# Layer normalisations of a feed-forward stage moved to ScalarE, attention masks cut to the outer thirds, and keys folded in 32-column pieces

## The reference, cut to what matters

```
def _layernorm(x, g, b): return (x - mu) * rsqrt(var + EPS) * g + b
valid = (abs(rel) <= w) & (k_pos >= 0) & (k_pos < S)
scores = where(valid, scores, -1e9); p = softmax(scores)
x = _layernorm(src + attn, ln1_g, ln1_b)
ff = maximum(x @ W1 + b1, 0.0) @ W2 + b2
return _layernorm(x + ff, ln2_g, ln2_b)
...
x = _layernorm(x + attention_layer(x))
q = einsum(x, w_q); q = (q - mean) * rsqrt(var + BN_EPS) * gamma + beta
sim = einsum('pbnhd,hkpd->pbnhk', q, keys)
```

## Time and profile before

| | us |
|---|---|
| median of 3 runs | 786.74 |
| lowest and highest | 784.21, 788.45 |
| profiled execution, its own time | 785.28 |
| span in the profile | 783.4 |
| busy PE, DVE, POOL, ACT | 624.2, 617.0, 435.2, 334.5 |

### The profile page before, as it was taken

One profiled execution on the slowest core, in us unless ns is written; L12 is line 12 of the kernel. 1 busy time (PEld: TensorE's weight loads), 2 busy tenths in 40 slices (PEclk: granted clock), 3 DMA queues, 4 the chain that ended last, 5 costly groups with the idle time before them and its releaser, 6 DMA issues.

```text
span 783.4 us, 46593 instructions
## 1 busy us (share of the span) xinstructions
PE 624.2 (80%) x19753; PEld 517.8 (66%) x19783; DVE 617.0 (79%) x1903; ACT 334.5 (43%) x514; POOL 435.2 (56%) x672
## 2 busy tenths in 40 slices
PE   5889989999988977877847487787877777777775
PEld 4667768778876855554645376676766666666674
DVE  3656747776766757999965888899999999999982
ACT  3434534545444452433320434455555455455540
POOL 4222422333232423554521778879888888898881
PEclk9999999999999998988975789999999999999997
DMA  6511111111111110000000122312222222222221
GB/s 171 196 32 38 30 29 30 37 33 35 33 36 28 34 54 14 15 28 13 0 8 3 40 62 64 70 41 67 67 67 67 64 64 67 67 67 51 58 61 41
DMA packets 45361, 38.81 MB, mean 50 GB/s; under 512 B 6512, under 2 KB 40432, under 8 KB 45040
## 3 DMA queue, kind: packets, MB, share of 16 engines
q1 hardware_dynamic: 45296, 37.86, 19.1%
HBM read 16.86 MB, written 2.10 MB: 24 GB/s over the span
## 4 chain that ended last, share of the span: by engine, by line
PE 41%; DVE 39%; issue 16%; POOL 1%; DVEq 1%; ACT 1%; DMA 1%; another core or an unknown queue 1%; SPq 0%; POOLq 0%; ACTq 0%
PE ps L640 12%; PE ps L653 8%; DVE top L1226 5%; PE ps L666 5%; DVE wq_sb L1257 4%; DVE prod L1281 3%; PE ps L635 3%; PE ps L806 3%; PE ps L827 3%; DVE hidT L1272 3%; DVE best L1237 2%; DVE stats L1040 2%; DVE x L1057 2%; DVE r_x L1266 2%; DVE r L1057 2%
## 5 line engine op out<-in xcount | busy, mean ns | idle before, releaser
L999 DVE TENSOR_REDUCE row_max<-ps 128x8 f32<-128x768 f32 x64 | 61.3, 958 | 77.2 <-PE ps L640 77.2
L827 PE MATMUL ps<-up_sb,prod 128*128 128x128 f32 x512 | 81.4, 322 | 46.7 <-DVE prod L1281 46.3
L462 POOL COPY v_ones<-v_raw 96x512 f32<-96x512 f32 x32 | 19.5, 609 | 168.5 <-DMA v_raw<-in_x_wrapped 168.5
L827 PEld LDWEIGHTS ps<-up_sb,prod 128*128 128x128 f32 x512 | 75.0, 229 | 53.4 <-DVE prod L1281 53.2
L864 ACT ACTIVATE arena<-arena 128x768 f32<-128x768 f32 x64 | 54.0, 844 | 125.9 <-DVE arena L1002 125.9
L640 PE MATMUL ps<-early 128*32 128x96 f32 x4096 | 102.4, 250 | 6.3 <-issue 6.3
L640 PEld LDWEIGHTS ps<-early 128*32 128x32 f32 x4096 | 86.8, 111 | 29.1 <-issue 29.1
L806 PE MATMUL ps<-arena,hidT 128*32 128x32 f32 x8192 | 82.0, 200 | 25.5 <-issue 20.8
L806 PEld LDWEIGHTS ps<-arena,hidT 128*32 128x32 f32 x8192 | 76.9, 112 | 31.0 <-issue 22.2
L557 POOL TENSOR_TENSOR wq_sb<-wq_sb,rel_exp 128x1024 f32<-128x1024 f32 x32 | 76.2, 2380 | 8.2 <-POOL rel_exp L553 7.2
L653 PE MATMUL ps<-ident,arena 128*96 128x128 f32 x512 | 70.0, 280 | 12.9 <-issue 7.6
(11 more groups left out here) (138 smaller groups left out, 1275.4 us busy)
## 6 DMA issues: line engine op xcount, KB each, us to landing
arena<-r_x SPq DMA_DIRECT2D x128, 128.0 KB, 2.4
v_raw<-in_x_wrapped SPq DMA_DIRECT2D x128, 48.0 KB, 1.8
arena<-in_x SPq DMA_DIRECT2D x8, 256.0 KB, 5.1
x_tile<-in_x SPq DMA_DIRECT2D x32, 64.0 KB, 1.8
x<-in_x SPq DMA_DIRECT2D x8, 256.0 KB, 2.8
xT_tile<-xT SPq DMA_DIRECT2D x32, 64.0 KB, 1.9
out<-out_tile SPq DMA_DIRECT2D x32, 64.0 KB, 1.5
wq_sb<-in_w_q SPq DMA_DIRECT2D x1, 1024.0 KB, 9.6
```

The lines of the kernel that those rows point to most:

```text
L827: mm = nc.tensor.matmul(ps[:, 6 + p, 0:P], pairs[:, c // 2, c % 2], up_sb[:, c, :], start=False, stop=(c == EC - 1))
L999: V.tensor_reduce(mx.rearrange("p (a b) -> p a b", a=2), sc, AX_X, ALU.max).then_inc(max_done, 1)
```

## The change

Three things are changed.

1. *Attention*: the mask matmuls come after the scores and cover only the outer thirds of each window, 256 columns in place of 384. The first score matmuls open the banks.
2. *Feed-forward*: (x - mean) * rstd becomes an ACTIVATE Identity with a scale and a shift column on ScalarE (`normalised`, four of 128x128 per norm). VectorE writes also -mean (`minus_mean`), GpSimd multiplies it by rstd (`ln_shift`) behind each power. VectorE keeps the multiply by g and the add (`ln1_affine`, `ln2_affine`; norm 3 has neither).
3. *Middle*: w_sim's products are cut into four 32-column pieces each, written to four 32-partition strips. The constant row of the first part goes to bank 0, so its splitting starts while TensorE still works on the second (`split_constants`), and ScalarE copies w_sim.

```diff
+        minus_mean = sb("minus_mean", [P, 12])
+        ln_shift = sb("ln_shift", [P, 12])
...
+                pool.wait_ge(rstd_done, k + 1)
+                hold(pool)
+                nc.gpsimd.tensor_tensor(ln_shift[:, 4 * lo:4 * hi], minus_mean[:, 4 * lo:4 * hi], rstd[:, 4 * lo:4 * hi],
+                                        ALU.mult).then_inc(shift_ready, 1)
...
-                for g in groups:
-                    nc.tensor.matmul(ps[:, g, 0:BLOCKS * WIN], ident_bf[:], mask[:, mask_at], start=True, stop=False,
-                                     skip_group_check=True)
                 for b in range(BLOCKS):
                     for g in groups:
                         for h in range(4):
                             mm = nc.tensor.matmul(ps[32 * h:32 * h + 32, g, b * WIN:(b + 1) * WIN], queries[p][:, b, h],
-                                                  windows[p][:, g, b * W:b * W + WIN], start=False, stop=True,
+                                                  windows[p][:, g, b * W:b * W + WIN], start=b == 0, stop=False,
                                                   skip_group_check=True)
-                        if b == BLOCKS - 1:
-                            mm.then_inc(scores_done, 1)
+
+                def edges_of(columns):
+                    return columns.rearrange("p (b s c) -> p b s c", s=3, c=W)[:, :, 0:3:2]
+
+                for g in groups:
+                    nc.tensor.matmul(edges_of(ps[:, g, 0:BLOCKS * WIN]), ident_bf[:], edges_of(mask[:, mask_at]),
+                                     start=False, stop=True, skip_group_check=True).then_inc(scores_done, 1)
...
-                nc.tensor.matmul(ps[:, 7, ks.start * KEYS:ks.stop * KEYS], ones[:],
+                nc.tensor.matmul(ps[:, 7 * part, ks.start * KEYS:ks.stop * KEYS], ones[:],
                                  keys_shifted[:, ks].rearrange("p a k -> p (a k)"), start=True, stop=True
                                  ).then_inc(c_row_done, 1)
                 for k in range(ks.start, ks.stop):
-                    mm = nc.tensor.matmul(ps[:, 6, k * KEYS:(k + 1) * KEYS], wqT_sb[:, k, :], keys_scaled[:, k, :],
-                                          start=True, stop=True)
+                    for g in range(4):
+                        mm = nc.tensor.matmul(ps[32 * g:32 * g + 32, 6, k * KEYS:(k + 1) * KEYS],
+                                              wqT_sb[:, k, 32 * g:32 * g + 32], keys_scaled[:, k, :],
+                                              start=True, stop=True)
             mm.then_inc(w_sim_done, 1)
-            pe.wait_ge(c_step, 5)
+            pe.wait_ge(c_step, 10)
...
+            def normalised(norm, src, dst, done):
+                for s in range(4):
+                    j = 4 * norm + s
+                    last = nc.scalar.activation(dst[:, s, :], src[:, s, :], ACT.Identity, bias=ln_shift[:, j:j + 1],
+                                                scale=rstd[:, j:j + 1])
+                last.then_inc(done, 1)
+
+            def ln1_norm(n, q, k, place=1):
+                a.wait_ge(shift_ready, k + 1)
+                need(a, ln_step, n)
+                need(a, x1_done, n)
+                normalised(place, r1[q], y2, ln1_normed)
+
+            def ln2_norm(n, k):
+                a.wait_ge(shift_ready, k + 1)
+                normalised(0, r2, r2, ln2_normed)
+
+            def ln3_norm(n, q, k):
+                a.wait_ge(shift_ready, k + 1)
+                need(a, gram_done, n - 1)
+                need(a, x3_kept, n - 1)
+                normalised(2, r3, x3[q][:, :, 0:P], x3_done)
+
             def stage(n, q):
                 a.wait_ge(r1_done, 4 * n + 4)
-                need(a, x1_done, n - 1)
+                need(a, ln1_normed, n - 1)
...
+                    if last:
+                        ln1_norm(p, p, 0, 1 + p)
...
                         stage(n + 2, q)
+                        ln1_norm(n + 2, q, 2 * n + 1)
+                    if not (first and q == 0):
+                        ln3_norm(n - 1, 1 - q, 2 * n + 1)
                     if not (last and q == 1):
                         hidden(n + 1)
+                    ln2_norm(n, 2 * n + 2)
                     if not (first and q == 0):
                         results(n - 1, 1 - q)
             over_pairs(a, NQ // 2, b2_act)
+            ln3_norm(NQ - 1, 1, 2 * NQ + 1)
...
+            a.wait_ge(w_sim_done, 1)
+            copy(w_sim[:], ps[:, 6, :]).then_inc(w_sim_copied, 1)
...
+                V.tensor_scalar(minus_mean[:, 4 * lo:4 * hi], moments[:, 4 * lo:4 * hi, 0], -1.0, None, ALU.mult)
                 V.tensor_scalar(var_eps[:, 4 * lo:4 * hi], moments[:, 4 * lo:4 * hi, 1], EPS, None, ALU.add
...
-            def ln_apply(norm, src, dst, done):
-                for a in range(4):
-                    j = 4 * norm + a
-                    last = V.tensor_scalar(dst[:, a, :], src[:, a, :], moments[:, j, 0:1], rstd[:, j:j + 1],
-                                           ALU.subtract, ALU.mult)
-                last.then_inc(done, 1)
...
-            def ln1_apply(n, q, place=1):
-                ln_apply(place, r1[q], y2, ln_step)
-                v.wait_ge(ln_step, 2 * n + 1)
+            def ln1_affine(n, q):
+                v.wait_ge(ln1_normed, n + 1)
                 V.tensor_tensor(y2[:], y2[:], bcast(ln1_g_all[:], 1, 4), ALU.mult).then_inc(ln_step, 1)
...
-            def ln2_apply(n, q):
-
-                ln_apply(0, r2, r2, r2_normed)
-                v.wait_ge(r2_normed, n + 1)
+            def ln2_affine(n, q):
+
+                v.wait_ge(ln2_normed, n + 1)
...
-                    v.wait_ge(rstd_done, 2 * n + 2)
                     if not last:
-                        ln1_apply(n + 2, q)
-                    if with_ln3:
-                        ln3_apply(n - 1, 1 - q)
-                    v.wait_ge(rstd_done, 2 * n + 3)
-                    ln2_apply(n, q)
+                        ln1_affine(n + 2, q)
+                    ln2_affine(n, q)
...
+            def split_constants(part):
+
+                cols = slice(Q_SPLIT[part].start * KEYS, Q_SPLIT[part].stop * KEYS)
+                c_rest = rel_exp[0][:].rearrange("p a k -> p (a k)")
+                v.wait_ge(c_row_done, part + 1)
+                V.tensor_copy(c_rows[:, cols], ps[:, 7 * part, cols]).then_inc(c_step, 1)
+                v.wait_ge(c_step, 5 * part + 1)
+                V.tensor_tensor(c_rest[:, cols], ps[:, 7 * part, cols], c_rows[:, cols], ALU.subtract).then_inc(c_step, 1)
+                v.wait_ge(c_step, 5 * part + 2)
+                V.tensor_copy(c_rows[2 * W:3 * W, cols], c_rest[2 * W:3 * W, cols]).then_inc(c_step, 1)
+                V.tensor_copy(c_rows[W:2 * W, cols], c_rest[W:2 * W, cols])
+                V.memset(c_rows[3 * W:P, cols], 0.0)
+                v.wait_ge(c_step, 5 * part + 3)
+                V.tensor_tensor(c_rest[2 * W:3 * W, cols], c_rest[2 * W:3 * W, cols], c_rows[2 * W:3 * W, cols],
+                                ALU.subtract).then_inc(c_step, 1)
+                v.wait_ge(c_step, 5 * part + 4)
+                V.tensor_copy(c_rows[2 * W:3 * W, cols], c_rest[2 * W:3 * W, cols]).then_inc(c_step, 1)
+
             for part in range(2):
                 scale_keys(part)
-            v.wait_ge(c_row_done, 2)
-            c_rest = rel_exp[0][:].rearrange("p a k -> p (a k)")
-            V.tensor_copy(c_rows[:], ps[:, 7, :]).then_inc(c_step, 1)
-            v.wait_ge(c_step, 1)
-            V.tensor_tensor(c_rest, ps[:, 7, :], c_rows[:], ALU.subtract).then_inc(c_step, 1)
-            v.wait_ge(c_step, 2)
-            V.tensor_copy(c_rows[W:2 * W, :], c_rest[W:2 * W, :])
-            V.memset(c_rows[3 * W:P, :], 0.0)
-            V.tensor_copy(c_rows[2 * W:3 * W, :], c_rest[2 * W:3 * W, :]).then_inc(c_step, 1)
-            v.wait_ge(c_step, 3)
-            V.tensor_tensor(c_rest[2 * W:3 * W, :], c_rest[2 * W:3 * W, :], c_rows[2 * W:3 * W, :], ALU.subtract).then_inc(c_step, 1)
-            v.wait_ge(c_step, 4)
-            V.tensor_copy(c_rows[2 * W:3 * W, :], c_rest[2 * W:3 * W, :]).then_inc(c_step, 1)
-            v.wait_ge(w_sim_done, 1)
-            V.tensor_copy(w_sim[:], ps[:, 6, :]).then_inc(w_sim_copied, 1)
+            for part in range(2):
+                split_constants(part)
```

More of the change, by code:

```diff
@@ L230, in attention_and_product_keys @@
         rstd_done = sem("rstd_done")
+        shift_ready = sem("shift_ready")
+        ln1_normed = sem("ln1_normed")
+        ln2_normed = sem("ln2_normed")
         ln_step = sem("ln_step")
@@ L244, in attention_and_product_keys @@
         gram_done = sem("gram_done")
-        r2_normed = sem("r2_normed")
         r2_scaled = sem("r2_scaled")
@@ L1063, in ln1_stats @@
                 return ln_stats(place, r1[q])
-            def ln1_apply(n, q, place=1):
-                ln_apply(place, r1[q], y2, ln_step)
-                v.wait_ge(ln_step, 2 * n + 1)
+            def ln1_affine(n, q):
+                v.wait_ge(ln1_normed, n + 1)
```

(9 more changed lines are left out.)

4 lines of the change are left out of this document (removed).

## The result

The changed kernel takes 822.7 us (median of four runs, 819.1 to 825.8) against 785.5 for the kernel before beside it: a ratio of the means of 1.047, 95% interval 1.041 to 1.053, or +36.8 us (the forecast was 818 us, its range 803 to 826). The profiled execution took 821.0 us with a span of 819.2; its own difference is 35.7 us where 32.6 were forecast.

| piece of the span, us | before | after | difference | forecast |
|---|---|---|---|---|
| to the first score matmul | 17.7 | 15.7 | -2.0 | 0 |
| first score to the x1T copy of quad 0 | 270.3 | 268.8 | -1.5 | -6.6 + 1.5 |
| that copy to the last ReLU of quad 1 | 20.9 | 25.7 | +4.8 | +2.8 |
| to the last ReLU of quad 7, six steps | 76.2 | 113.4 | +37.2 | +40.1 |
| to the gram's second moment | 20.2 | 19.5 | -0.7 | -0.8 |

What follows compares the result with a forecast made beforehand. The prediction took VectorE to bound the feed-forward stage and TensorE attention. From 785.3 us, masks -6.6, feed-forward +43.6 and middle -4.4 gave 818 us (817.9), range 803 to 826.

Steps and rivals of the forecast that it cites:

- The ring: Feed-forward: ReLUs queue on ScalarE behind a statistics round trip that depends on the previous quad's ReLUs; step 20.6 us against 12.7.
- The norm group: Feed-forward: four 128x128 normalising ACTIVATEs on ScalarE, forecast at 1.5 us, with ends of 0.97 and 1.83.
- The start: Feed-forward entry: norm 1 of quad 0 ahead of the last probability copies, +1.5 us; quad 1 waits for staged statistics, +2.8.
- The tail: End of feed-forward, from the last ReLU to the gram's second moment: 19.4 us against 20.2 before, so -0.8.
- The masks: Attention: 256 mask columns in place of 384 save 0.11 us per half tile, -6.6 us in all (0 to -9).
- The middle: Between feed-forward and last stage: earlier splitting of the constant row lets TensorE go on sooner, -4.4 us (-2.5 to -5.5).
- (a): Rival, feed-forward: TensorE's clock stays up, 1.8 us less for quads 2 to 7, total 807 us; chance 0.14.
- (b): Rival, feed-forward: ScalarE's norm groups lie at an end of their cost range, total 809 or 824 us; chance 0.12.
- (c): Rival, attention: mask matmuls cost as before, columns not being what they pay for, total 825 us; chance 0.09.
- (d): Rival, feed-forward: faster, VectorE sheds work and norms fall into ScalarE's waits, step 11.1 us, total 765; chance 0.03.
- (e): Rival, feed-forward: no change in time, a step of about 14 us with the statistics round trip overlapped; chance 0.02.

## Why the prediction came out right

**The ring, and its length.** The step was forecast as a sum of eight pieces. In the step shown above they are, forecast first: products and transposes 4.44 and 4.44; x3T copies 0.84 and 0.93; staging copy 0.73 and 0.66; statistics 1.01 and 1.03; moments with hand-overs 1.15 and 1.10; power and shift 2.18 and 2.06; two norm groups 3.1 and 3.09; x1T copy to last ReLU 7.14 and 7.16. Sum 20.6 and 20.5. Almost every piece was read from before, because the ring uses no work that before did not have, bar the norms and the small shift. That the norms' place ahead of the ReLUs closes it is shown by the order alone (norms behind the ReLUs: 12.3 us). The staging copy's place is worth less than the prediction made of it: with the copy early the ring closes over norm 2 and VectorE, at 18.2 to 19.2 us. Six steps: 113.4 us against 116.3 forecast. The 2.9 missing are 0.8 in quad 2, 0.3 in each of quads 3 to 6, and 0.7 in quad 7, where the pieces of a full step were carried over to steps that lack some. In quads 2 and 7 some 0.4 of it is the first layer, 6.7 us from x1T copy to last ReLU in place of 7.14.

**The total** fits better than its terms, and that part is luck. In the profiled executions the difference is 3.1 us above the forecast: attention with the start of the kernel 1.6 more than forecast, the first two quads 2.0 more, the middle 0.8 more and the untouched last stage 1.6 more, against 2.9 less in the six steps. The two largest errors of the changed stages have opposite signs.

**The norm group** was sized a little too low: 1.5 forecast, 1.64 to 1.65 measured. An estimate from the figures of the Trainium skill ("ScalarE: Activation LUTs", section "What ACT_TABLE_LOAD costs") had given 1.64 for a group and 479 ns for a single one, beside a measured mean of 481: the trace agrees, and here the page was better than my estimate from the nearest row. In the ring the effect was small, since neighbouring groups overlap by 0.1 too, which I had booked as 0.1 the other way. The row, count and mean of one in ns:

```profile
L887 ACT ACTIVATE y<-r_x,ln_shift,rstd 128x128 f32<-128x128 f32 x32 | 13.1, 481 | 31.4 <-POOL ln_shift L481 31.4
```

**The start** is where a step failed: +2.8 forecast for quads 0 and 1 up to the last ReLU, +4.8 measured. Quad 1's extra wait was 2.4 where 2.8 were priced. Missing was quad 0: its first layer, 5.26 us from x1T copy to last ReLU before, took 7.85. Norm 1 of quad 0 stands on ScalarE from 276.90 to 278.44 ahead of the last tile's probability copies, TensorE has then idled 2.78 us when it goes on at 279.15, and the granted clock over the first layer of quad 0 was 0.61, against 1.00 before. The norm and the pause, then TensorE alone in the window over that layer, of the kernel after and of the kernel before:

```profile
276.90 1.63 ACT L887 ACTIVATE y<-r_x,ln_shift,rstd 128x128 f32<-128x128 f32 x4
...
279.15 1.91 PE L663 MATMUL ps<-ident,arena 128*96 128x128 f32 x8 [2.78 <-ACT arena L860]
```

```profile
284.50:292.50 8.00, 6.61 (x9) 0.61 0.00 0
```

```profile
288.00:293.50 5.50, 4.12 (x10) 1.00 0.16 48
```

I had asked for the clock in the ring and not at its entrance. That the norm is the cause is borne out by the other kernels, with one exception. In each of the six others with this norm on ScalarE TensorE idles 2.5 to 2.8 us there, and quad 0 takes 6.9 to 8.1 us; without it quad 0 takes 5.3 us in the kernel before and three others, but 6.7 with the masks alone, where the pause is 0.92 us. Why the clock fell in that one stays open.

**The tail** took 19.5 us against 19.4.

**The masks** were forecast at -6.6, from a third of 0.33 us in each half tile. The times give -5.3 (-2.6 to -8.1). The columns do pay: between the two kernels that differ in nothing else a mask pair takes 0.10 us less, and the round 0.08 us less per half tile, where 0.11 was forecast. An undisturbed pair of tiles went from 15.4 to 14.9 us in all, which is 0.13 per half tile, and 0.05 of that came with the place, which the prediction had put at nothing. Over the whole stage the kernels with the new masks show less gain than that, and where the rest goes stays open.

**The middle** was forecast at -4.4; the trace shows -3.6 in the kernel after and -3.9 alone. 0.4 us of the missing lies ahead of the constant row, where q's moments took 9.6 us in place of 9.2 since TensorE's clock rose later: in the first 2.2 us it was granted 0.72 in place of 0.92, and the products of q's moments took 4.25 us in place of 3.84. The rest lies behind it. TensorE, VectorE and ScalarE in the middle of the kernel after, against the earlier trace rows:

```profile
452.69 1.33 PE L787 MATMUL ps<-keys_shifted,ones 128*128 128x288 f32 x2 [5.01 <-DVE keys_shifted L1215]
...
453.95 1.19 PE L792 MATMUL ps<-keys_scaled,wqT_sb 128*32 128x32 f32 x72
454.20 0.45 DVE L1230 CAST c_rows<-ps 128x288 bf16<-128x288 f32 x1
...
457.16 0.60 ACT L860 ACTIVATE w_sim<-ps 128x512 f32<-128x512 f32 x1 [15.01 <-PE ps L792]
...
459.27 1.22 PE L803 MATMUL ps<-w_sim,xT_tile 128*128 128x512 f32 x1 [2.18 <-DVE c_rows L1241]
```

72 records take 1.19 us, 16 to 17 ns each, where I took 24. That made TensorE earlier and gained nothing, since VectorE ends last: from its first cast to the similarities it took 459.27 - 454.20 = 5.07 us, in two rounds of seven small instructions, where 4.6 were forecast. The step that was mis-sized is this splitting. From constant row to similarities it makes 6.6 us, against 10.6 before and 6.2 forecast.

**The rivals.** (a) did not happen, and its price was right when it was made to happen. (b)'s upper end, 824 us, can't be told from the measured time, and its lower end, 809, is out. (c) is out: the pair takes 0.33 us with 256 columns and 0.43 with 384. (d) was right that the norms can fall into ScalarE's waits, and wrong in two points. It hung on the staging copy's place, but the early copy alone left the step at 18 to 19 us; the norms' place decides. And its 765 us was too good, since GpSimd's work goes on holding VectorE when the norms leave it; the lowest ratio seen, 0.984, is some 773 us. (e) did not happen: the ring of the change takes 20.1 to 20.5 us, not 14.

## What to carry to other kernels

Before work is moved to an idle engine, write down that engine's program order and ask of each instruction behind the new one whether it now waits for something it had nothing to do with; if the thing waited for depends on an earlier round of the same queue, add up the ring, and the ring is the step. Here the same instructions on the same engine gave a kernel 5% slower or 1.3% faster by their place in the queue, and of the 1.3% about half came with the other two parts of the change. A ring with a pause also costs the clock, so price TensorE's work after each new pause, the first one included, at what the trace shows for it after a pause. And when a ring is opened, look for the next round that closes: here it ran over VectorE and GpSimd, with 2.9 of its 12.3 us spent in VectorE instructions held up by GpSimd.

## What the hardware showed that was not expected

**GpSimd holds VectorE's two-input instructions as well.** I had looked only at the single-input L1057 (2.78 us for four, 1.11 otherwise) and expected the stalls to go with it. They did not. The add of b was already held in the kernel before, 1.64 us in six of its eight steps, and stayed held in seven of eight after; the multiply by g, 0.69 us in every step before, took 1.80 in three of the eight steps after. The groups of the kernel after (count, busy us, mean ns of one):

```profile
L1109 DVE TENSOR_TENSOR r_x<-y,ln_b_all 128x512 f32<-128x512 f32 x8 | 12.5, 1566 | 0.3
...
L1105 DVE TENSOR_TENSOR y<-y,ln_g_all 128x512 f32<-128x512 f32 x8 | 8.9, 1108 | 10.7 <-ACT y L887 10.7
...
L1122 DVE TENSOR_TENSOR r<-r,ln_g_all 128x512 f32<-128x512 f32 x8 | 5.5, 692 | 53.4 <-ACT r L887 53.4
...
L1114 DVE TENSOR_TENSOR r<-ps,x_b 128x512 f32<-128x512 f32 x8 | 5.5, 687 | 0.0
```

Same shape, same kind: 692 ns where GpSimd is idle, a mean of 1566 for the add that mostly stands beside its adds, and 687 for the one with an input in PSUM, which in the step above ran beside GpSimd's power (376.07 and 376.33). The Trainium skill, "SBUF — State Buffer", section "Who interferes with whom", says that a VectorE instruction with two SBUF inputs contends with a GpSimd instruction that reads SBUF, and one with at most one SBUF input does not, outside the 2-port modes. The rows agree: in the step with the norms behind the ReLUs the multiply ends at 347.65, 0.55 us after GpSimd's add that began beside it, and the next add at 349.33, again 0.55 after GpSimd's next one. That the one with a PSUM input would also go free beside GpSimd's adds no run here shows. ScalarE's norms never stretched: 477 to 494 ns for each of the 96.

**The slow first layer has no single length.** With the clock up the eight matmuls took 3.9 us in every kernel. With it down they took 5.3 to 6.5 in the change (5.7 at a granted 0.64 in the step shown, 6.5 for its quad 0) and up to 6.8 in the other kernels. A price of "the slow layer" from one row can be 1 us off.

**The attention stage wanders.** With the same instructions, its length from the first score to the first x1T copy differs by up to 5.1 us between profiles (268.8 to 273.9 in the six with the new masks and ScalarE's first norm, of which the change itself is the shortest), at least in part in stalls inside TensorE's blocks that the chain of waits lists as issue (8.8% of it in the change, 9.4 to 10.6% in three others). What they are stayed open. A gain of 2 to 4 us is best read from its own place in the trace.
